# Four more row tiles on TensorE, four fewer on GpSimd, in a message-passing kernel on one core

## The chip, the core and the metric

The kernel runs on one core of one Trainium2 chip. The metric is the device time of one execution, in microseconds (us), as the median of several runs. A core has five engines that run their own instruction streams and wait for each other through semaphores: TensorE (PE in the profile, with its weight loads as PEld), VectorE (DVE), ScalarE (ACT), GpSimd (POOL), and SyncE (SP), which here only issues DMAs.

## The reference

A graph network layer: 6,250 nodes with 64 features, 206,250 edges sorted by their target node `dst`. For each edge the source node's row is fetched, the edge's features are added, and the result is clipped at zero. The messages are summed into their target nodes, and two dense layers follow.

```python
h = jnp.maximum(_layernorm(x, axis=-1), 0.0)
# _L0_gnn_ref(h, edge_index, edge_attr_64, W1, b1, W2, b2):
msg = jax.nn.relu(x[src] + edge_attr)
agg = jax.ops.segment_sum(msg, dst, num_segments=x.shape[0])
h = x + agg
h = jax.nn.relu(h @ W1 + b1)
return h @ W2 + b2
# and around it
x = x + _L0_gnn_ref(h, ...)
```

## The kernel before

**Tiling.** The edges are cut into 124 chunks of 1,664. A chunk is 13 tiles: a tile holds one edge on each of the 128 partitions, 64 features wide. Chunks are numbered (t, u): 31 turns t of `SLOTS` = 4 slots u, and each slot has its own buffer `gath`. Only the fetching of the source rows (`x[src]`) is spread over several engines, and the change is about this spread.

**Three ways to fetch a tile's source rows.**

- GpSimd gathers them from the table `h_table` in DRAM with one indirect DMA a tile (L392, `gather_rows`). `pool_tiles(t, u)` says how many tiles of a chunk it gets.
- TensorE picks them out of a copy of the table in on-chip memory, by multiplying with one-hot matrices. `pe_tiles(t, u)` says how many. For one tile these are 7 key blocks times two halves of the table (`table_hi`, `table_lo`), so 14 matmuls of 128x448 into one PSUM bank `ps_cand` (L1294, `candidates`). ScalarE makes the one-hot matrices `keyhot` for a whole chunk: seven `Abs` passes (L735) and one `Relu` pass over all of them (L742), into one of two buffers, `u % 2`. VectorE multiplies each tile's bank with a mask (L966, `picked`), which frees the bank, and sums over the seven candidates (L973, into `gath`).
- SyncE fetches 20 tiles in the whole run as 128 small DMAs each, one a row (L515, 2,560 of them). These 20 tiles are the "row tiles", one in each of 20 chunks that `ROW_CHUNKS` lists. `row_tiles(t, u)` is 1 there and 0 elsewhere.

What one way takes, GpSimd's share loses: `pool_tiles` is 13 less the two others. A chunk without a row tile has 4 tiles on TensorE and 9 on GpSimd. In `PE_SPARED`, every fifth row chunk, TensorE has 3, GpSimd 9 and SyncE 1. These four chunks are (5, 1), (12, 2), (19, 3) and (27, 0). In the other 16 row chunks TensorE has 4 and GpSimd 8. Chunk (0, 0) has none on TensorE.

**Order.** It is written out by hand. TensorE runs the candidates of two chunks, then the scatter matmuls (L421) of two earlier ones; in each turn a first dense layer (L445) follows behind chunk (t, 1), and a second (L455) behind chunk (t, 2). ScalarE starts on the keys of a chunk when TensorE has finished the chunk before the last one, since the `keyhot` buffer is free then. In slot 3 it first does the relu of the first layer (L450), which waits for L445. Before the keys of each chunk it copies the edge features of another one to PSUM (L723). VectorE adds gathered rows and edge features (L1014), splits them by target (L1021, L1031) and adds the scattered sums (L1082). TensorE waits for two things ahead of a tile: the chunk's keys, and that VectorE has masked the tile four tiles back, which used the same bank (`bank_uses_before`). GpSimd waits for VectorE's sum of the chunk four back, and its gathers are held to within two chunks of TensorE's progress by `released` (L631), through the semaphore `cands_ready`, whose count is 8 ahead.

**End.** The last chunk's sum is done in two pieces (L1052), of which the second waits for GpSimd's last three gathers. The two last pieces of the dense layers come behind them.

Of the kernel before, what the change touches and what calls it, by code (L numbers as in the profile page):

```python
# [70 lines left out]
PE_MAX = 4  # L71
# [12 lines left out]
def row_chunk(k):  # L84

    half = -(-P * (k + 1) // sum(ROWS_AT)) - 1
    return half // PAIRS + 1, half % PAIRS * PAIR + (k + 1) % PAIR


ROW_CHUNKS = [row_chunk(k) for k in range(ROW_TILES)]  # L90
PE_SPARED = ROW_CHUNKS[2::5]
assert (TURNS - 1, SLOTS - 1) not in ROW_CHUNKS and len(set(ROW_CHUNKS)) == ROW_TILES
assert len(PE_SPARED) % PE_MAX == 0
KEY_BLOCKS = N_GROUPS
KEYS_BEHIND = 1
POOL_LOW = 3
# [10 lines left out]


def pe_tiles(t, u):
    return PE_MAX - int((t, u) in PE_SPARED) if (t, u) != (0, 0) else 0  # L110


def row_tiles(t, u):
# [3 lines left out]
def pool_tiles(t, u):  # L117
    return TILES_PER_CHUNK - pe_tiles(t, u) - row_tiles(t, u)


def pe_before(t, u, i=0):
    return sum(pe_tiles(c // SLOTS, c % SLOTS) for c in range(t * SLOTS + u)) + i
# [37 lines left out]
def build(nc, x_nodes, x_cols, x_t, src_t, src_rows, src_keys, src_cands, dst_t, base_t, edges_t, w1, b1, w2, b2, out):  # L160
# [9 lines left out]
    with ExitStack() as ctx:  # L170
# [431 lines left out]
        def _(pool):  # L602
# [21 lines left out]
            def gather_chunk(t, u):  # L624
                if (t, u) == (1, 0):
                    pool.wait_ge(late_idx_loaded, 16)

                pool.wait_ge(summed, t * SLOTS + (u + 1))

                n, m, k = pool_tiles(t, u), pe_tiles(t, u), row_tiles(t, u)  # L630
                released = {i * n // m: pe_before(t, u, i) + 1 for i in range(m)}  # L631
                if not alone(t, u):
                    gather_rows(slot_rows(t, u)[:, k:, :], idx_all[:, t * SLOTS + u, k:], n, gathered[u], released)
                    return

                early = n - END_LATE
                gather_rows(slot_rows(t, u)[:, m:, :], idx_all[:, t * SLOTS + u, m:], early, gathered[u],
                            {r: count for r, count in released.items() if r < early})
                gather_rows(slot_rows(t, u)[:, END_EARLY:, :], idx_all[:, t * SLOTS + u, END_EARLY:], END_LATE, gathered_late,
                            {r - early: count for r, count in released.items() if r >= early})  # L640
# [827 lines left out]
```

## Time and profile before

| | |
|---|---|
| median of 3 runs | 1407.31 us (1406.56 to 1408.48) |
| the profiled execution: its own time | 1406.28 us |
| its span, from the first to the last instruction | 1404.5 us |
| PE busy | 1367.9 us, 97% of the span |
| PEld busy | 710.0 us, 51% |
| DVE busy | 1213.3 us, 86% |
| ACT busy | 1069.0 us, 76% |
| POOL busy | 1054.4 us, 75% |

The busy time is the time in which an engine had at least one instruction under way. Matmuls overlap each other, so the duration of one matmul is longer than its distance to the next. Idle time is shown with what ended it. "issue" means that the profile shows nothing that the engine waited for. The views are in one execution's own time, from the first instruction at 0.

### The profile page before, as it was taken

The page shows a single profiled execution, that of the slowest core. Times are in us where ns is not written, and L with a number is a line of the kernel's source. Part 1 is how long each engine was busy: PE and PEld are TensorE (multiplying, and loading weights), DVE is VectorE, ACT ScalarE, POOL GpSimd, SP SyncE. Part 2 cuts the span into 40 slices and gives each one's busy share as a digit, 9 for nine tenths or more (in the row PEclk, how much of TensorE's full clock was granted, in tenths as well). Part 3 has the DMA queues.
Part 4 walks back from the last instruction along what each step waited for, and adds up shares of the span by engine and source line. Part 5 has one row for each costly group of instructions (what it writes and reads, how often), then busy time and mean ns, then how long its engine had stood idle before and what let it go on. Part 6 is the DMA issues. An engine that isn't in the chain of part 4 may idle for free.

```text
span 1404.5 us, 26571 instructions
## 1 busy us (share of the span) xinstructions
PE 1367.9 (97%) x7780; PEld 710.0 (51%) x7780; DVE 1213.3 (86%) x1867; ACT 1069.0 (76%) x1166; POOL 1054.4 (75%) x1113
## 2 busy tenths in 40 slices
PE   6787999999999999999999999999999999999998
PEld 5443555555555555555555555555555555555554
DVE  7688988888888888888888888888888888888887
ACT  6685877787777877778777787787877778787773
POOL 6777777777777777777777777777777777777775
PEclk9999999999999999999999999999999999999999
DMA  7222332332332323323233232332332323323221
GB/s 255 57 58 64 87 95 72 85 89 65 94 87 71 87 67 94 87 70 92 69 87 87 70 92 65 91 91 66 94 85 69 93 65 94 86 69 94 66 83 30
DMA packets 70785, 116.54 MB, mean 83 GB/s; under 512 B 34522, under 2 KB 35950, under 8 KB 70638
## 3 DMA queue, kind: packets, MB, share of 16 engines
q1 hardware_dynamic: 34302, 76.39, 17.2%
q0 software_dynamic: 35328, 36.25, 13.3%
q10 hardware_dynamic: 1008, 2.19, 0.5%
q8 instruction: 62, 1.02, 0.3%
q14 instruction: 85, 0.70, 0.2%
HBM read 111.39 MB, written 3.34 MB: 82 GB/s over the span
## 4 chain that ended last, share of the span: by engine, by line
PE 91%; DVE 5%; ACT 2%; DMA 1%; issue 0%; DVEq 0%; SPq 0%; ACTq 0%
PE ps_cand L1294 88%; PE ps L421 2%; ACT keyhot L735 1%; ACT keyhot L742 1%; DVE gath L973 1%; DVE parts L1021 1%; DVE picked L966 1%; PE ps L455 1%; DVE ends L1031 1%; DVE ps_edge L1014 0%; PE ps_cand L1250 0%; PE ps L445 0%; DMA key_pair<-key_table 0%; ACT agg L715 0%; DVEq L1070 0%
## 5 line engine op out<-in xcount | busy, mean ns | idle before, releaser
L392 POOL DMA_INDIRECT gath<-h_table,idx_all x1091 | 1040.4, 954 | 333.9 <-issue 311.4
L1294 PE MATMUL ps_cand<-table_hi,keyhot 128*128 128x448 f16 x3388 | 1197.9, 354 | 20.5 <-DVE picked L966 16.6
L1294 PE MATMUL ps_cand<-table_lo,keyhot 128*128 128x448 f16 x3388 | 1197.1, 353 | 0.0
L735 ACT ACTIVATE keyhot<-key_pair,key_bias 128x512 f16<-128x512 f16 (+1 forms) x854 | 532.7, 705 | 133.3 <-PE ps_cand L1294 131.4
L1294 PEld LDWEIGHTS ps_cand<-table_hi,keyhot 128*128 128x128 f16 x3388 | 332.0, 98 | 334.3 <-issue 15.1
L1294 PEld LDWEIGHTS ps_cand<-table_lo,keyhot 128*128 128x128 f16 x3388 | 332.2, 98 | 302.3 <-issue 2.9
L742 ACT ACTIVATE keyhot<-keyhot,hot_bias 128x3584 f16<-128x3584 f16 (+1 forms) x122 | 397.4, 3258 | 4.0
L966 DVE TENSOR_TENSOR picked<-ps_cand,cand_mask 128x448 f32<-128x448 f32 x488 | 302.5, 620 | 101.2 <-PE ps_cand L1294 100.9
L973 DVE TENSOR_REDUCE gath<-picked 128x64 f32<-128x448 f32 x488 | 299.2, 613 | 4.1
L1021 DVE SCALAR_TENSOR_TENSOR parts<-ps_edge,side 128x832 f32<-128x832 f32 x242 | 235.5, 1015 | 0.0
L1031 DVE TENSOR_REDUCE ends<-parts 128x128 f32<-128x1664 f32 x122 | 229.0, 1877 | 0.0
L723 ACT ACTIVATE ps_edge<-edge_pair 128x832 f32<-128x832 f32 x123 | 106.0, 862 | 58.7 <-DVE parts L1021 58.6
L1014 DVE TENSOR_TENSOR ps_edge<-gath,ps_edge 128x832 f32<-128x832 f32 x122 | 124.5, 1020 | 25.6 <-ACT ps_edge L723 12.6
L450 ACT ACTIVATE part_z<-ps,b_sb 128x96 f32<-128x96 f32 x29 | 9.9, 341 | 94.2 <-PE ps L445 90.2
L1082 DVE TENSOR_TENSOR agg<-agg,ps 128x64 f32 x124 | 27.5, 222 | 40.1 <-DVE agg L1082 37.5
L980 DVE TENSOR_TENSOR onehot<-iota_f,place 128x128 f32<-128x128 f32 x124 | 35.0, 282 | 0.0
L421 PEld LDWEIGHTS ps<-onehot,ends 128*64 128x64 f32 x488 | 19.2, 136 | 22.7 <-issue 22.6
L421 PE MATMUL ps<-onehot,ends 128*64 128x64 f32 x488 | 27.8, 234 | 0.0
L619 POOL DMA_INDIRECT gath<-x_nodes,idx_all x13 | 12.8, 983 | 7.5 <-DMA idx_all<-src_t 3.9
L450 ACT ACTIVATE end_z<-ps_cand,b_sb 128x240 f32<-128x240 f32 (+1 forms) x2 | 0.8, 408 | 19.5 <-PE ps_cand L445 19.5
L715 ACT ACTIVATE agg<-ps 64x512 f32<-64x512 f32 (+1 forms) x8 | 7.1, 995 | 10.1 <-PE ps L1262 10.1
L455 PE MATMUL ps<-part_z,w_sb 64*64 64x96 f32 x116 | 11.1, 268 | 0.0
(108 smaller groups left out, 185.3 us busy)
## 6 DMA issues: line engine op xcount, KB each, us to landing
edge_pair<-edges_t SPq DMA_DIRECT2D x62, 832.0 KB
gath<-h_table SPq DMA_DIRECT2D x2560, 0.2 KB
gath<-h_table,idx_all POOLq DMA_INDIRECT x1091, 2.4
key_pair<-key_table SPq DMA_DIRECT2D x61, 256.0 KB
h_table<-h_a SPq DMA_DIRECT2D x7, 224.0 KB, 2.8
part_x<-x_t SPq DMA_DIRECT2D x29, 48.0 KB
out<-part_out SPq DMA_DIRECT2D x29, 48.0 KB
x_c<-x_cols ACTq DMA_DIRECT2D x4, 256.0 KB, 4.9
```

What stands on the lines that cost most here:

```text
L392: nc.gpsimd.indirect_dma_start(out=rows[:, r, :], out_offset=None, in_=h_table, in_offset=bass.IndirectOffsetOnAxis(ap=idx[:, r:r + 1], ax ...
L421: last = nc.tensor.matmul(bank[k * D:(k + 1) * D, :], ends[u][:, k, :], onehot[u][:, k, :], start=True, stop=True)
L723: nc.scalar.activation(edge_near, edge[u], ACT.Copy).then_inc(edge_copied, 1)
L735: last = nc.scalar.activation(keyhot[u % 2][:, a, 0:n], key[u][:, P * PE_MAX - n:], ACT.Abs, bias=key_bias[:, a:a + 1])
L742: nc.scalar.activation(keyhot[u % 2][:, :, 0:n], keyhot[u % 2][:, :, 0:n], ACT.Relu, bias=hot_bias[:, 0:1], scale=-1.0 / SCALE).then_inc(a ...
L966: nc.vector.tensor_tensor(picked[i][:, :, :], ps_cand[cand_bank(t, u, i)][:, 0:D * CAND].rearrange("p (d b) -> p d b", b=CAND), mask.to_br ...
L973: nc.vector.tensor_reduce(slot_rows(t, u)[:, column, :], picked[i][:, :, :], AX_X, ALU.add).then_inc(selected, 1)
L980: nc.vector.tensor_tensor(onehot[u][:, :, :], iota_f[:, 0:WIN].unsqueeze(1).to_broadcast([P, ENDS, WIN]), place[:, bass.ds(c, 1), :].rearr ...
L1014: nc.vector.tensor_tensor(edge_near if near(t, u) else edge_sum, slot_rows(t, u), edge_near if near(t, u) else edge[u], ALU.add).then_inc( ...
L1021: last = nc.vector.scalar_tensor_tensor(out=parts[:, k, :, :], in0=(edge_near if near(t, u) else edge_sum).rearrange("p r d -> p d r"), sc ...
L1031: nc.vector.tensor_reduce(ends[u][:, :, :], parts[:, :, :, :], AX_X, ALU.add).then_inc(ends_ready, 1)
L1294: last = nc.tensor.matmul(bank[:, 0:D * CAND], keyhot[u % 2][:, a, i * P:(i + 1) * P], half[:, a, :, :].rearrange("p d b -> p (d b)"), sta ...
```

## The change

TensorE gets four tiles in every chunk but the first, the four chunks of `PE_SPARED` included, and the list is gone. In these four chunks GpSimd's share falls from 9 tiles to 8. In numbers: four tiles move from GpSimd to TensorE.

```diff
@@ -88,9 +88,7 @@
 ROW_CHUNKS = [row_chunk(k) for k in range(ROW_TILES)]
-PE_SPARED = ROW_CHUNKS[2::5]
 assert (TURNS - 1, SLOTS - 1) not in ROW_CHUNKS and len(set(ROW_CHUNKS)) == ROW_TILES
-assert len(PE_SPARED) % PE_MAX == 0
 KEY_BLOCKS = N_GROUPS
@@ -107,7 +105,7 @@
 def pe_tiles(t, u):
-    return PE_MAX - int((t, u) in PE_SPARED) if (t, u) != (0, 0) else 0
+    return PE_MAX if (t, u) != (0, 0) else 0
```

The lines of the changed kernel are numbered two lower than those of the kernel before. The order in which instructions are issued moves only inside the four chunks; (5, 1) stands for all. On GpSimd, the gathers of chunk (5, 1) (into `gath1`) before:

```order
L392 DMA gath1<-h_table,idx_all 128x64 [waits cands_ready,summed]
L392 DMA gath1<-h_table,idx_all 128x64 x2
L392 DMA gath1<-h_table,idx_all 128x64 [waits cands_ready]
L392 DMA gath1<-h_table,idx_all 128x64 x2
L392 DMA gath1<-h_table,idx_all 128x64 [waits cands_ready]
L392 DMA gath1<-h_table,idx_all 128x64 x2
```

And the same chunk in the changed kernel:

```order
L390 DMA gath1<-h_table,idx_all 128x64 [waits cands_ready,summed]
L390 DMA gath1<-h_table,idx_all 128x64
L390 DMA gath1<-h_table,idx_all 128x64 [waits cands_ready]
L390 DMA gath1<-h_table,idx_all 128x64
L390 DMA gath1<-h_table,idx_all 128x64 [waits cands_ready]
L390 DMA gath1<-h_table,idx_all 128x64
L390 DMA gath1<-h_table,idx_all 128x64 [waits cands_ready]
L390 DMA gath1<-h_table,idx_all 128x64
```

Nine gathers have become eight, released in four steps where there were three. On VectorE, the part that handles TensorE's candidates of chunk (5, 1) before, from the second tile on:

```order
L966 TENSOR_TENSOR picked1<-ps_cand1,cand_mask 128x448 [waits cands_ready]
L1021 SCALAR_TENSOR_TENSOR parts<-ps_edge,side 128x832 [waits summed]
L1021 SCALAR_TENSOR_TENSOR parts<-ps_edge,side 128x832
L973 TENSOR_REDUCE gath1<-picked1 128x64 [waits masked]
L966 TENSOR_TENSOR picked2<-ps_cand2,cand_mask 128x448 [waits cands_ready]
L1031 TENSOR_REDUCE ends0<-parts 128x128 [waits parted]
L973 TENSOR_REDUCE gath1<-picked2 128x64 [waits masked]
L980 TENSOR_TENSOR onehot1<-iota_f,place 128x128 [waits scattered]
```

And in the changed kernel:

```order
L964 TENSOR_TENSOR picked1<-ps_cand1,cand_mask 128x448 [waits cands_ready]
L1019 SCALAR_TENSOR_TENSOR parts<-ps_edge,side 128x832 [waits summed]
L1019 SCALAR_TENSOR_TENSOR parts<-ps_edge,side 128x832
L971 TENSOR_REDUCE gath1<-picked1 128x64 [waits masked]
L964 TENSOR_TENSOR picked2<-ps_cand2,cand_mask 128x448 [waits cands_ready]
L1029 TENSOR_REDUCE ends0<-parts 128x128 [waits parted]
L971 TENSOR_REDUCE gath1<-picked2 128x64 [waits masked]
L964 TENSOR_TENSOR picked3<-ps_cand3,cand_mask 128x448 [waits cands_ready]
L971 TENSOR_REDUCE gath1<-picked3 128x64 [waits masked]
L978 TENSOR_TENSOR onehot1<-iota_f,place 128x128 [waits scattered]
```

A mask and a sum for the fourth tile have come in. TensorE's own stream gains the 14 matmuls of that tile in each of the four chunks, ahead of whatever stood behind the third. The assignment of banks `ps_cand` is shifted by one between spared chunks before, and is not after; each tile still waits for the one four back. ScalarE's passes for these chunks go from 384 to 512 columns a block. SyncE's stream is the same.

## Rows read from the trace of the kernel before

**Rows 1.** Chain that ended last, by engine and then by line, whole span.

```profile
PE 91%; DVE 5%; ACT 2%; DMA 1%; issue 0%; DVEq 0%; SPq 0%; ACTq 0%
```

**Rows 2.** Busy time in stretches: stretch, length, engines' busy us, PEclk, DMA.

```profile
140.00:260.00 120.00, 120.00 (x678) 61.74 (x677) 108.17 (x164) 95.00 (x103) 90.72 (x97) 1.00 0.32 85
260.00:580.00 320.00, 320.00 (x1809) 164.71 (x1808) 279.93 (x426) 249.93 (x275) 241.91 (x257) 1.00 0.32 82
580.00:620.00 40.00, 39.54 (x226) 20.30 (x225) 36.07 (x54) 30.71 (x34) 30.25 (x33) 1.00 0.32 81
620.00:1215.00 595.00, 595.00 (x3363) 306.14 (x3361) 519.52 (x789) 465.07 (x506) 449.88 (x477) 1.00 0.31 81
1215.00:1393.00 178.00, 178.00 (x1011) 91.62 (x1009) 155.49 (x238) 129.22 (x140) 134.44 (x143) 1.00 0.29 72
```

**Rows 3.** Waits from 140 to 1393 us: total us, times, longest.

```profile
PE ps_cand L1294 <- ACT keyhot L742: 0.5, 1, 0.5
POOL gath L392 <- issue: 286.3, 939, 0.3
...
POOL gath L392 <- PE ps_cand L1294: 17.4, 57, 0.3
DVE ps_edge L1014 <- DMA gath<-h_table,idx_all: 12.2, 11, 2.7
```

**Rows 4.** Chain in order of time, pairs of chunks with 7 or 8 TensorE tiles.

```profile
260.91 18.64 PE ps_cand L1294 x98
...
302.20 21.29 PE ps_cand L1294 x112
...
1220.08 18.64 PE ps_cand L1294 x98
```

**Rows 5.** Chain around (19, 3): slot 2 with four tiles, slot 3 with three.

```profile
893.08 10.70 PE ps_cand L1294 x56
903.78 0.31 PE ps L455 x4
904.09 8.05 PE ps_cand L1294 x42
```

**Rows 6.** Chain around (12, 2) and (12, 3).

```profile
588.80 4.32 ACT keyhot L735 x7
593.12 0.02 issue
593.14 3.29 ACT keyhot L742
596.43 0.04 issue
596.48 10.77 PE ps_cand L1294 x56
```

**Rows 7.** ScalarE in order of time, around (12, 2) and (12, 3).

```profile
576.61 3.65 ACT L735 ACTIVATE keyhot<-key_pair,key_bias 128x384 f16<-128x384 f16 x7 [1.97 <-PE ps_cand L1294]
580.29 2.54 ACT L742 ACTIVATE keyhot<-keyhot,hot_bias 128x2688 f16<-128x2688 f16 x1
587.70 0.34 ACT L450 ACTIVATE part_z<-ps,b_sb 128x96 f32<-128x96 f32 x1 [4.88 <-PE ps L445]
587.94 0.86 ACT L723 ACTIVATE ps_edge<-edge_pair 128x832 f32<-128x832 f32 x1
```

**Rows 8.** Groups: busy us, mean ns of one, idle before.

```profile
L392 POOL DMA_INDIRECT gath<-h_table,idx_all x1091 | 1040.4, 954 | 333.9 <-issue 311.4 <-PE ps_cand L1294 18.3 <-DVE ps_edge L1014 2.4
L1294 PE MATMUL ps_cand<-table_hi,keyhot 128*128 128x448 f16 x3388 | 1197.9, 354 | 20.5 <-DVE picked L966 16.6 <-ACT keyhot L742 3.8
L966 DVE TENSOR_TENSOR picked<-ps_cand,cand_mask 128x448 f32<-128x448 f32 x488 | 302.5, 620 | 101.2 <-PE ps_cand L1294 100.9
L973 DVE TENSOR_REDUCE gath<-picked 128x64 f32<-128x448 f32 x488 | 299.2, 613 | 4.1
```

**Rows 9.** GpSimd and VectorE in order of time, at the end.

```profile
1394.28 0.95 POOL L392 DMA_INDIRECT gath<-h_table,idx_all  x1 [0.30 <-issue]
1395.54 0.94 POOL L392 DMA_INDIRECT gath<-h_table,idx_all  x1 [0.30 <-issue]
...
1398.70 0.22 DVE L1082 TENSOR_TENSOR agg<-agg,ps 128x64 f32 x1 [0.21 <-DVE agg L1082]
1398.84 0.35 DVE L1052 TENSOR_TENSOR ps_edge<-gath,ps_edge 128x192 f32<-128x192 f32 x1
```

**Rows 10.** DMA issues by line: KB each, median us from issue to landing.

```profile
gath<-h_table,idx_all POOLq DMA_INDIRECT x1091, 2.4
```

**Rows 11.** Waits from 30 to 160 us, TensorE on VectorE.

```profile
PE ps_cand L1294 <- DVE picked L966: 16.6, 4, 7.0
```

## The prediction, made before the changed kernel ran

> **What bounds the kernel now.** Four tiles move from GpSimd to TensorE, so the first question is which of the two the end waits for. I read the chain that ended last first: 91% of the span lies on TensorE [rows 1]. A share over the whole run can hide stages, so the next view is the busy time in stretches. From 140 us to 1393 us TensorE is busy in every microsecond but 0.46: the stretches 140 to 580 and 620 to 1393 are full, and the one between has 39.54 of 40 us [rows 2]. The waits of the same time agree: TensorE waited once, 0.5 us, for ScalarE's keys, and never for VectorE, a gather or a bank [rows 3]. All four places of the change lie there. (5, 1) is in the pair of chunks that starts at 260.91 [rows 4], (12, 2) runs just before the gap at 596 [rows 6], (19, 3) starts at 904.09 [rows 5], and (27, 0) is in the other stretch of 98 matmuls, at 1220.08 [rows 4]. The granted clock is 1.00 in all of these stretches, the full 2.4 GHz level.
>
> GpSimd looks nearly as full as TensorE. One gather takes 954 ns and is followed by 0.3 us of "issue" [rows 3, 8], and the last two start 1.26 us apart [rows 9]; with the 0.94 us of most gathers the distance is about 1.25 us. So 1,091 gathers make 1,091 x 1.25 = 1,364 us. But its own waits on TensorE, 17.4 us in 57 pieces [rows 3], show it held back by TensorE, not the other way. VectorE waits for landed gathers 12.2 us in 11 pieces [rows 3], and not one of these reaches TensorE.
>
> **The change part by part.**
>
> TensorE, added: 4 tiles of 14 matmuls, 56 in all. Two pairs of rows give the price of one tile. A pair of chunks with 8 tiles takes 21.29 us and one with 7 takes 18.64 [rows 4], a difference of 2.65. A chunk with 4 takes 10.70 and one with 3 takes 8.05 [rows 5], again 2.65. The mean of 354 ns for a matmul [rows 8] is not the price, because neighbours overlap: 21.29 us for 112 is 190.1 ns from start to start, and 14 x 190.1 = 2.66. I take 2.65 x 4 = 10.60 us. Nothing hides it, since TensorE has no idle time at these places.
>
> Here a rule speaks for a smaller price. The Trainium skill, page "TensorE: Matmul & The Clock Gate", section "Back-to-back issue gap", gives about 131 ns for a matmul of 512 columns in a sustained stream of weight loads and matmuls; by that, as an estimate, 56 matmuls would add at most 7.3 us. The trace disagrees, with 190.1 ns at 448 columns.
>
> TensorE, taken away: the gap of 0.46 us. It exists because (12, 2) has three tiles. ScalarE cannot begin the work for (12, 3) before the first layer's relu, which it could run at 587.70, when TensorE started (12, 2) [rows 7]. The relu, the copy and the keys end at 596.43 [rows 6], and three tiles plus the second layer's 0.31 us [rows 5] end at 587.7 + 8.05 + 0.31 = 596.0. With four tiles TensorE comes to the same point at 598.7, and ScalarE has 2.3 us to spare. So -0.46 us. The three other places have no gap to give back [rows 2].
>
> ScalarE, added: 128 more columns a block. For (12, 2) it needed 3.65 + 2.54 us [rows 7] and for the full (12, 3) 4.32 + 3.29 [rows 6], 1.4 us more. Cover: it then sat idle 4.88 us until L445 [rows 7]. At the other places no relu stands ahead of the next keys' way, and ScalarE already makes full keys for 118 other chunks (124 less the first two and these four); from 140 us on TensorE waits for none but (12, 3). Cost 0; without its cover, 1.4 us a place.
>
> VectorE, added: one mask of 0.62 us and one sum of 0.61 us a place [rows 8]. It is busy 279.93 of 320 us [rows 2], so it has 1.4 us idle in each 11 us chunk, and TensorE needs the result only four tiles later, 10.6 us on. Queued behind the added pair are the window's one-hot and the accumulation, and the scatter waits for those. The same sequence with a row tile, four TensorE tiles and eight gathers runs in 16 chunks of the kernel before, and TensorE never waits in them. Cost 0. The bound from above is the wait that the trace shows where VectorE is really late: 16.6 us in 4 pieces near the start [rows 11], where VectorE does work of its own between the chunks. Nothing of that kind is near these places, so I take the lower end.
>
> GpSimd, taken away: 4 x 1.25 = 5.0 us. It is off the chain, and what it gains it spends waiting for TensorE's `released`. At the end its last gather starts at 1395.54 [rows 9] and lands 2.4 us later [rows 10], at 1397.9. The sum that needs it starts at 1398.84, with no idle time before it, directly behind the accumulation at 1398.70 [rows 9]. So the gathers are 0.9 us early as things are, and earlier ones shorten nothing. Worth 0.
>
> The shifted banks cost nothing: the distance of four tiles is kept, and four spared tiles brought the count back to the same bank at the end.
>
> Sum: 10.60 - 0.46 = **+10.1 us**. Made on the profiled execution: 1406.28 + 10.1 = 1416.4. That execution lies 1.03 us under the median of the runs, so for the median 1407.31 + 10.1 = **1417.4 us**.
>
> **The rivals.**
>
> *GpSimd sets the pace, and the kernel gets faster.* GpSimd would be the engine behind which everything queues, and TensorE's added tiles would fall into time that it spends waiting. For: its 1,364 us of gathers in a span of 1404.5, and VectorE's 12.2 us of waits for them. Then four gathers fewer give -5.0 us: 1402.3. It decides from the point at which TensorE waits 2.65 us or more at each place; the trace has 0.46 us at one place and 0 at three. Chance 3%.
>
> *TensorE has room that its busy share hides, and nothing changes.* Busy time counts overlapping matmuls of 354 ns, and its weight loads fill only 164.71 of 320 us [rows 2]. If the matmuls were spaced by something else (the weight loads' order, a port), a further tile would slip in between: 1407.3. Against it: a stretch with 14 matmuls more takes 2.65 us more in both pairs of rows, where it should then take the same. Chance 3%. The Trainium skill, page "Perfetto Trace Analysis", section "Identifying the Most-Contended Engine", says that matmul busy time is a poor measure and to use the share of LDWEIGHTS; by it TensorE, at 51%, would be behind VectorE and GpSimd. The trace disagrees: a tile's price shows in full.
>
> *A new wait comes on top.* At the four places TensorE finds keys or a bank late, because ScalarE and VectorE got more to do there. The nearest row is the gap of 0.5 us [rows 3]; one at each place makes 4 x 0.46 = 1.8 us, and the old gap stays with them or is one of them: 10.6 + 1.8 = 12.4, so 1419.7. Against it: 119 full chunks without a wait. Chance 5%.
>
> **How the numbers follow.** The forecast has 89%. Its own range: the price of the tiles is between 10.6 and 10.65 us (56 x 190.1 ns). From below, each place might give back as much as (12, 2) does, 1.8 us in all: +8.8. From above, nothing is given back: +10.65. With the runs' own scatter, 0.8 us down and 1.2 us up, this is 1415.4 to 1419.2, and I use 1415.3 to 1419.2. It leaves out the two small cases and most of the third, about 1 in 10. The difference that a measurement of this kernel can tell from none is about 0.2%, 2.8 us. Slower by more than that: the forecast and the new wait, 94%. Within it: 3%. Faster: 3%.
>
> **What would show it right or wrong.** In the changed kernel's trace every slot pair of the loop takes 21.29 us with 112 matmuls and none has 98. TensorE's wait for keys at 596 is gone, and its busy time has grown by 10.6 us. GpSimd has 1,087 gathers, the same 1.25 us apart, and waits more for TensorE's tiles. The stretch behind the last candidate matmul is as long as before, 11.5 us. I am wrong if TensorE shows waits for VectorE's masks or for keys at the four places, if the stretch at the end shrinks by more than a microsecond (then the gathers had set it), or if a pair with 112 matmuls there takes less than 21.29 us.

## The result, and the profile after

The changed kernel took 1417.04 us (median of 6 runs, 1415.35 to 1418.08), the kernel before 1406.49 us on the same chip (6 runs, 1405.74 to 1408.48). The ratio is 1.0074, with a 95% interval of 1.0064 to 1.0084: slower by 10.5 us, which in the interval's bounds is 9.0 to 11.8. The forecast was +10.1, 1417.4 us.

The busy time in stretches of the changed kernel, to be held against [rows 2]. Columns as there: stretch, its length, busy us of PE, PEld, DVE, ACT and POOL, granted clock, DMA share, GB/s.

```profile
140.00:260.00 120.00, 120.00 (x684) 61.73 (x682) 107.80 (x164) 95.16 (x104) 90.44 (x97) 1.00 0.31 81
260.00:580.00 320.00, 320.00 (x1804) 164.69 (x1803) 279.14 (x425) 249.36 (x271) 241.90 (x257) 1.00 0.31 82
580.00:620.00 40.00, 40.00 (x229) 20.59 (x228) 34.43 (x54) 32.24 (x35) 30.21 (x32) 1.00 0.32 86
620.00:1215.00 595.00, 595.00 (x3361) 306.15 (x3361) 519.27 (x785) 462.02 (x501) 449.54 (x476) 1.00 0.31 81
1215.00:1402.00 187.00, 187.00 (x1060) 96.26 (x1060) 162.41 (x250) 136.85 (x148) 132.15 (x140) 1.00 0.27 70
```

TensorE is now busy in every microsecond from 140 to 1402. The third row has lost the 0.46 us gap. The chain in order of time, from its parts at the four places and the end (start, us, what):

```profile
259.81 21.29 PE ps_cand L1292 x112
...
589.20 10.70 PE ps_cand L1292 x56
599.89 0.31 PE ps L453 x4
600.21 10.70 PE ps_cand L1292 x56
...
907.76 10.70 PE ps_cand L1292 x56
...
1226.39 21.29 PE ps_cand L1292 x112
...
1402.13 0.27 PE ps L419 x4
```

These answer to [rows 4], [rows 5] and [rows 6]. The two pairs with 98 matmuls in 18.64 us have become pairs with 112 in 21.29; the slot 3 with 42 in 8.05 has become 56 in 10.70; and (12, 3) starts at 600.21 right behind the second layer, with no keys of ScalarE in the chain. The keys of (12, 3) were ready 2.2 us before TensorE came to them, since ScalarE's last pass for them runs from 594.68 to 597.96:

```profile
594.68 3.28 ACT L740 ACTIVATE keyhot<-keyhot,hot_bias 128x3584 f16<-128x3584 f16 x1
```

From the start of the pair with (5, 1) to the end of the last candidate matmul it is 1402.13 - 259.81 = 1142.32 us, and before, where the last candidate matmul ends at 1393.17, it was 1393.17 - 260.91 = 1132.26: **+10.06 us**. The stretch behind the last candidate is 11.4 us, and was 11.3. The whole span has grown by only 9.0 us, since this execution reached the pair 1.10 us earlier; that part lies ahead of the change's first place.

What I had not foreseen is in the gathers. One line's summary of GpSimd's gathers, first before the change, then after (durations in ns min/median/max, start of the first and of the last in us):

```profile
L392 POOL DMA_INDIRECT gath<-h_table,idx_all x1091: 940/944/3984, 23.7 to 1395.5; - x182
```

```profile
L390 POOL DMA_INDIRECT gath<-h_table,idx_all x1087: 939/944/3141, 22.3 to 1388.6; - x182
```

GpSimd starts its last gather 6.9 us earlier, while TensorE's last candidate ends 9.0 us later. In the kernel before, 1,090 steps from gather to gather took 1371.8 us. The usual step is 1.25 us, and the rest comes from 19 gathers that took more than 1 us, up to 3.98. No pause between two gathers was longer than 0.32 us, so TensorE did not hold GpSimd back anywhere. In the changed kernel it did once, ahead of the change's first place, for 1.19 us where the usual pause is 0.30:

```profile
131.53 0.94 POOL L390 DMA_INDIRECT gath<-h_table,idx_all  x1 [1.19 <-PE ps_cand L1292]
```

One more pause there, of 0.59 us at 156.8, has nothing that the profile shows behind it. From 157 us to the end there is none over 0.32. VectorE's 12.2 us of waits for gathers [rows 3] are gone from the changed kernel.

### The profile page after: what moved, and what is told of

It is laid out like the page before. It is cut to its first block, busy times and chain, and to the rows that moved or that the text cites. A ratio compares the mean times of both kernels' runs of the same rounds, so it can differ in the third digit from the quotient of the medians.

```text
span 1413.5 us, 26687 instructions
## 1 busy us (share of the span) xinstructions
PE 1379.5 (98%) x7836; PEld 714.4 (51%) x7836; DVE 1218.8 (86%) x1875; ACT 1075.0 (76%) x1166; POOL 1048.6 (74%) x1109
## 4 chain that ended last, share of the span: by engine, by line
PE 93%; DVE 5%; ACT 1%; DMA 1%; issue 0%; DVEq 0%; SPq 0%; ACTq 0%
PE ps_cand L1292 89%; PE ps L419 2%; DVE gath L971 1%; DVE parts L1019 1%; PE ps L453 1%; DVE picked L964 1%; DVE ends L1029 1%; DVE ps_edge L1012 0%; PE ps L443 0%; DMA key_pair<-key_table 0%; ACT keyhot L733 0%; PE ps_cand L1248 0%; ACT agg L713 0%; DVEq L1068 0%; DVE h_a L868 0%
## 5 line engine op out<-in xcount | busy, mean ns | idle before, releaser
L733 ACT ACTIVATE keyhot<-key_pair,key_bias 128x512 f16<-128x512 f16 x854 | 535.8, 709 | 144.9 <-PE ps_cand L1292 143.8
L740 ACT ACTIVATE keyhot<-keyhot,hot_bias 128x3584 f16<-128x3584 f16 x122 | 400.4, 3282 | 4.0
```

The lines of the kernel that those rows point to most:

```text
L733: last = nc.scalar.activation(keyhot[u % 2][:, a, 0:n], key[u][:, P * PE_MAX - n:], ACT.Abs, bias=key_bias[:, a:a + 1])
L740: nc.scalar.activation(keyhot[u % 2][:, :, 0:n], keyhot[u % 2][:, :, 0:n], ACT.Relu, bias=hot_bias[:, 0:1], scale=-1.0 / SCALE).then_inc(a ...
```

## The experiments

**One half of the change at a time.** The first kernel takes only the gathers away. In the four spared chunks one tile is then not fetched at all, and its rows are stale.

```diff
 def pool_through(t, u):
-    return sum(pool_tiles(k, u) for k in range(t + 1))
+    return sum(pool_tiles(k, u) - int((k, u) in PE_SPARED) for k in range(t + 1))
...
-                n, m, k = pool_tiles(t, u), pe_tiles(t, u), row_tiles(t, u)
+                n, m, k = pool_tiles(t, u) - int((t, u) in PE_SPARED), pe_tiles(t, u), row_tiles(t, u)
```

> The kernel before, with 488 tiles on TensorE, and in the four spared chunks one gather fewer on GpSimd (1,087), so that one tile of each of these chunks is left unfetched and its rows are stale. This is GpSimd's half of the change alone. If TensorE sets the end, the time is that of the kernel before, within 1 us, though GpSimd's last gather starts 5 us earlier. If GpSimd sets the pace, it is 5.0 us faster.

Measured: 1406.60 us (11 runs) against 1406.73 (22 runs of the kernel before on the same chip, with which the next three kernels are compared too), ratio 0.9999, 0.999 to 1.0008. In us, here and below, that is the ratio taken times the kernel before: -0.1 (-1.4 to +1.1). The last gather starts at 1391.1 in place of 1395.5. Four gathers fewer give nothing that can be told from zero, and not the 5.0 us of the rival, so GpSimd did not set the pace.

The second kernel is the changed one with the four gathers put back, as idle work.

```diff
+EXTRA = ROW_CHUNKS[2::5]
...
 def pool_through(t, u):
-    return sum(pool_tiles(k, u) for k in range(t + 1))
+    return sum(pool_tiles(k, u) + int((k, u) in EXTRA) for k in range(t + 1))
...
                     gather_rows(slot_rows(t, u)[:, k:, :], idx_all[:, t * SLOTS + u, k:], n, gathered[u], released)
+                    if (t, u) in EXTRA:
+                        gather_rows(gath_wide[u][:, TILES_PER_CHUNK:, :], idx_all[:, t * SLOTS + u, n:], 1, gathered[u])
```

> The changed kernel, with 492 tiles on TensorE, and in the same four chunks one more gather on GpSimd, into a column that nothing reads (1,091 gathers, as before). This is TensorE's half of the change alone. If TensorE sets the end: 1417.0 us, as the changed kernel, +10.5 on the kernel before. If the fewer gathers had given something back in the changed kernel, this one is slower than it, by up to 5.0 us.

Measured: 1416.48 us (5 runs), ratio to the kernel before 1.0070, 1.0056 to 1.0084, which is +9.8 us (7.9 to 11.8). The whole effect is there with GpSimd's work as before. The two halves are 0 and the whole: the tiles on TensorE are the cause.

**How near GpSimd was.** The same idle gathers, added to the kernel before (`PE_SPARED` in place of `EXTRA`):

> The kernel before with one more gather in each of the four spared chunks, into a column that nothing reads (1,095 gathers, TensorE unchanged). My prediction read GpSimd as held back by TensorE; the order in time shows it running without a pause from 23.7 to 1396.5 us, with its last rows 0.9 us ahead of the sum that needs them. If it was held back and has room: no change. If it runs free and is only 0.9 us short of the end: 5.0 - 0.9 = 4.1 us slower, with VectorE waiting for gathers at the last sum.

Measured: 1411.42 us (6 runs), ratio 1.0032, 1.0020 to 1.0044: +4.5 us (2.8 to 6.2), against 4.1 expected. VectorE in order of time, at the end of that kernel:

```profile
1399.78 0.83 DVE L1054 TENSOR_TENSOR ps_edge<-gath,ps_edge 128x640 f32<-128x640 f32 x1 [0.86 <-DMA gath<-h_table,idx_all]
...
1402.54 0.22 DVE L1084 TENSOR_TENSOR agg<-agg,ps 128x64 f32 x1 [0.21 <-DVE agg L1084]
1403.52 0.36 DVE L1054 TENSOR_TENSOR ps_edge<-gath,ps_edge 128x192 f32<-128x192 f32 x1 [0.76 <-DMA gath<-h_table,idx_all]
```

Both pieces of the last sum now wait for gathers. In [rows 9] the same second piece followed the accumulation without idle time. With four gathers fewer the time is the same, with four more it is 4.5 us longer: the kernel before stands just short of GpSimd's bound.

The lateness is not the whole price. TensorE waited 3.7 us for VectorE's split (`parts`), which waited for the late rows, and behind that wait its granted clock is 0.50, the lower of its two levels, 1.2 GHz. The chain's last scatter matmuls, and the stretch that they lie in (columns as in [rows 2]):

```profile
1402.35 3.18 PE ps L1309 x52
```

```profile
1403.00:1408.00 5.00, 3.79 (x54) 2.87 (x50) 2.01 (x7) 0.35 (x1) 0.00 (x0) 0.50 0.07 25
```

In the kernel before the same 52 matmuls took 1.98 us (1.39 + 0.59), with TensorE waiting 1.7 us ahead of them and a granted clock of 1.00 from 1398.5 to 1402.6. The profiled execution of the kernel with idle gathers is the slowest of its six runs; its span is 7.1 us longer than that of the kernel before. The second piece of the last sum starts 4.7 us later (1403.52 against 1398.84), the work from there to the end of VectorE's last instruction takes 0.8 us more, and the last output lands 1.6 us later still. So the 4.5 us fit the 4.1 expected, but the expectation had no term for the clock.

**The opposite of the change.** Eight spared chunks, none of them in slot 2.

```diff
-PE_SPARED = ROW_CHUNKS[2::5]
+PE_SPARED = [c for c in ROW_CHUNKS if c[1] != 2][::2]
```

> The opposite of the change: eight chunks with three tiles on TensorE (484 tiles) and 1,095 gathers, none of the eight in slot 2. If TensorE alone sets the end: 4 x 2.65 less, 10.6 us, and the 0.46 us gap gone too, -11.1 on the kernel before (1395.4). If GpSimd is full to within 0.9 us: it ends 5.0 us later and TensorE no longer matters, +4.1 (1410.6).

Measured: 1411.09 us (11 runs), ratio 1.0030, 1.0021 to 1.0039: +4.2 us (3.0 to 5.5). The idle gathers alone cost as much. TensorE had 10.6 us less to do than there, and it made no difference. Then all twenty row chunks, `PE_SPARED = ROW_CHUNKS`:

> All twenty row chunks spared by TensorE (three tiles there, 472 in all), and 1,107 gathers, 16 more than before. If TensorE set the end, it would be 16 x 2.65 = 42 us faster. If GpSimd's free run sets it: 16 x 1.25 = 20.0, less the 0.9 us that it has to spare, +19.1 on the kernel before, with TensorE idle for some 60 us in waits for VectorE's masks.

Measured on another chip: 1427.81 us (4 runs) against 1408.45 (7 runs), ratio 1.0141, 1.0122 to 1.0160: +19.9 us (17.2 to 22.5), against 19.1. The cause stands, but the waits are not where I put them. Who waited for whom from 140 to 1412 us (total us, times, longest):

```profile
ACT ps_edge L723 <- DVE parts L1021: 224.1, 96, 4.6
DVE ps_edge L1014 <- DMA gath<-h_table,idx_all: 112.2, 58, 3.7
...
PE ps_cand L1294 <- ACT keyhot L742: 42.5, 29, 3.8
```

TensorE waits 42.5 us for ScalarE's keys (I had put the wait at some 60 us), not for VectorE's masks. The gathers are late, so VectorE's sums are; ScalarE's copy of the next edges waits for VectorE, and the keys stand behind that copy on ScalarE.

**The gap.** Two kernels move the spared chunks, four in each.

```diff
-PE_SPARED = ROW_CHUNKS[2::5]
+PE_SPARED = [c for c in ROW_CHUNKS if c[1] == 2][:4]
```

> Still four spared chunks and 1,091 gathers, but all four in slot 2: (3, 2), (6, 2), (9, 2), (12, 2). If the 0.46 us gap comes from the relu that holds back the keys of slot 3 behind a slot 2 with three tiles, there are four gaps of about 0.46 us, 1.8 in all. If the gap at (12, 2) was an accident of that one place, there is one or none.

TensorE's waits of that kernel from 140 to 1390 us:

```profile
PE ps_cand L1294 <- ACT keyhot L742: 1.9, 4, 0.5
```

Four gaps, 1.9 us in all. Its one run took 1409.47 us, within the 1406.02 to 1411.92 us that the kernel before took on that chip (7 runs, median 1408.45), so its time says nothing about the gaps. The other kernel has `PE_SPARED = [(5, 1), (11, 1), (19, 3), (27, 0)]`.

> The kernel before with the spared chunk (12, 2) replaced by (11, 1). By the same theory of the gap, TensorE has no wait from 140 us to the last candidate and is busy in every microsecond; by the rival, a spared chunk anywhere near there leaves a gap of about 0.5 us.

From 140 to 1390 us TensorE has no wait at all. The gap belongs to a slot 2 with three tiles. Yet the one run of this kernel took 1412.05 us. Its gathers, the same 1,091:

```profile
L392 POOL DMA_INDIRECT gath<-h_table,idx_all x1091: 941/947/4012, 23.5 to 1398.7; - x182
```

and VectorE's waits behind 1390 us:

```profile
DVE ps_edge L1052 <- DMA gath<-h_table,idx_all: 2.4, 1, 2.4
```

The last gather starts 3.2 us later than in the profile of the kernel before. Its median of 947 ns, against 944, is not the whole reason: the gathers took 1.9 us more in sum, and two pauses near the start took more than the usual 0.3 us, 1.38 us (for TensorE, at 134.2) and 0.60 (at 159.5). VectorE waits 2.4 us for late rows, and the second piece of the last sum starts 3.0 us later, at 1401.88. The rest of the 5.8 us by which the span is longer is not GpSimd's directly: 0.8 us in the work behind, with a granted clock of 0.67 from 1401.0 to 1406.4, and 1.9 us until the last output had landed. In the kernel with four gaps the median was 947 ns too and the last gather started later still, at 1398.9, but no piece of the last sum waited for it, because TensorE's candidates ended at 1396.3, not 1394.1. Which of the two engines is last is decided by a microsecond or two, and with one run of each I can say so of these executions only.

**Relief for both.** If TensorE and GpSimd are both full, only a third engine can help. SyncE gets 24 row tiles, 8 spared, so that GpSimd keeps its 1,091 gathers.

```diff
-ROWS_AT = (28, 16)
+ROWS_AT = (32, 20)
...
-PE_SPARED = ROW_CHUNKS[2::5]
+PE_SPARED = ROW_CHUNKS[1::3]
```

> A third engine takes part of the load: SyncE fetches 24 row tiles (32 and 20 rows a half turn in place of 28 and 16), eight of them are spared by TensorE (484 tiles) and GpSimd has 1,091 gathers, as before. TensorE's work is 10.6 us less than before. If GpSimd's free run is the second bound, 0.9 us short of the first: only 0.9 us faster, which can't be told from no change. If SyncE can't issue eight more rows in each 22 us (it had 183.7 us of waits for VectorE's sums in the whole run, for 512 more DMAs of 0.36 us each, 184 us): slower, with VectorE waiting for rows.

Measured: 1464.83 us (5 runs) against 1407.12 (9 runs), ratio 1.0413, 1.0399 to 1.0427: +58 us. Who waited for whom in it, on the engines and (last row) on SyncE's queue:

```profile
ACT keyhot L735 <- DMA key_pair<-key_table: 271.9, 49, 7.5
...
PE ps_cand L1294 <- ACT keyhot L742: 57.0, 38, 4.9
```

```profile
SPq L533 <- DVE ps_edge L1014: 26.2, 4, 15.5
```

SyncE was left with 26.2 us of waits for VectorE where the kernel before had 183.7, so it is full. What comes late is not the rows, as I had expected, but the keys' load (L527), which stands behind the rows on SyncE's queue; ScalarE waits 271.9 us for it, and TensorE for ScalarE. With 26 row tiles (34 and 22 rows; `ROW_CHUNKS[1::3][:8]` spared):

> The same with 26 row tiles (34 and 22 rows), eight spared, and GpSimd at 1,089 gathers: by GpSimd's run 2.5 + 0.9 = 3.4 us faster than before. But SyncE needs 768 more DMAs of 0.36 us, 276 us, where it had 184 us of waits: 92 us too many, so 90 us slower if SyncE then sets the pace.

Measured: 1760.62 us (5 runs), ratio 1.2513, 1.2496 to 1.2531: +354 us, nearly four times my 90. ScalarE waited 539.1 us for the keys' load and VectorE 152.3 us for `part_x`, both SyncE's. Why do two more row tiles cost so much more than the first four? Not by the rows' own DMAs, which follow each other every 0.33 us on average in all three kernels. Ahead of every group of at most 16 rows (`ROWS_A_LOAD`) SyncE loads their addresses into registers (L510), and my 0.36 us a row left most of their time out. These loads before, and with 26 row tiles (durations in ns, as above):

```profile
L510 SPq TENSOR_LOAD <-row_at x187: 491/1166/1342, 32.4 to 1319.5; - x187
```

```profile
L510 SPq TENSOR_LOAD <-row_at x297: 719/1247/3696, 32.0 to 1718.9; - x149
```

In sum they took 202 us before, 252 with 24 row tiles (247 loads) and 481 with 26. Of the 297 loads of the last kernel 56 took more than 3 us, 197 us together; in the two others none takes over 1.5. With them SyncE's account comes out within 10 us. For 26 row tiles: 768 rows x 0.333 = 256 us, and 279 for the loads, less the 171 us of waits that were used up, make 364, and 354 were measured. For 24: 171 + 50 - 158 = 63, and 58 were measured. Why those 56 loads took so long is open. The mean granted clock was 0.918 in its profiled execution, with TensorE waiting 271.8 us, and 0.992 in the changed kernel's. No version measured here beats the kernel before.

## Why the prediction was right, and where its reasons were not

- **TensorE's tiles, +10.60 us.** Right. All four places changed from 18.64 to 21.29 or from 8.05 to 10.70 as the two pairs of rows said, and with GpSimd's work held as before, the kernel is still 9.8 us slower.
- **The gap, -0.46 us.** Right in place and cause. It is gone in the changed kernel; four spared chunks in slot 2 make four of them, four in other slots none. ScalarE's keys were ready 2.2 us early, as against the 2.3 forecast. Together with the piece behind it, which ran 0.07 us longer after the gap, it explains why the stretch grew by 10.06 and not 10.60.
- **ScalarE and VectorE at nothing.** Right: TensorE waits for neither from 140 us to its last candidate.
- **GpSimd's gathers at nothing.** The size is right (0.9999 with four gathers fewer), and so is one reason: the last rows landed 0.9 us ahead of the sum that needs them. The other reason is not. I read "17.4 us in 57 pieces" [rows 3] as GpSimd held back by TensorE. But those pieces are 0.3 us each, as long as the 939 pieces put down to "issue": the same pause behind every gather, credited to a semaphore that happened to be near in time. In the kernel before GpSimd ran free from its first gather to its last. That it would spend its gain on waiting is refuted too: its last gather started 6.9 us earlier, 1.4 of it from an earlier start.
- **The end.** Right: 11.4 us against 11.3. The 0.9 us by which the last rows were early [rows 9, 10] turned out to be the most important number of the profile, though the forecast needed it only for a zero. It is about all that GpSimd had to spare: the four idle gathers, 5.0 us of work, cost 4.5 us. With an interval of 2.8 to 6.2 and the lower clock at the end in it, that does not measure the 0.9 itself.
- **The rivals.** "GpSimd sets the pace" is refuted for this change by the kernel with fewer gathers, but GpSimd's bound was nearer than a chance of 3% suggests: a bound 0.9 us away does nothing in one direction and sets the time at once in the other. "TensorE has room" is refuted by the changed kernel with idle gathers, and no new wait appeared.

## What to carry to other kernels

Where two engines share divisible work, find each one's free-running end before moving a piece: here one tile more on TensorE costs 2.65 us. One gather more on GpSimd costs about its 1.25 us once 0.9 us in all are used up. Four gathers fewer gave nothing, and four tiles fewer on TensorE gave nothing beside four more gathers, because the other engine is within a microsecond. Such a change is best split on the chip into its halves, with idle work on one side; two kernels then say whose time it is. Count also what an engine does between the pieces of work: most of SyncE's address loads were left out of its price per row, and they are over half of what the last experiment added to it. And look at the longest of a group of waits, not only their sum: if it equals the engine's ordinary pause, there is no sign that anything was waited for.

## What the runs showed of the hardware

An indirect gather of 128 rows of 256 bytes holds GpSimd for 944 ns in the median and is followed by 0.30 us of idle time even when the profile shows nothing that the next one waits for. On another chip the median was 947 ns in three kernels. A candidate matmul of 448 columns in a stream with a weight load ahead of each started every 190.1 ns at the full granted clock, in every stretch of 112 that was looked at, before and after. After a wait of 3.7 us near the end TensorE's granted clock was 0.50, and 52 scatter matmuls took 3.18 us in place of 1.98; after one of 1.7 us it was still 1.00. Small DMAs from SyncE, 256 bytes each, were issued every 0.33 us, and the register load ahead of at most 16 of them took 1.2 us in the median, but over 3 us in 56 of 297 cases in the kernel with 26 row tiles.
